# A LayerNorm / RWKV / mixture-of-experts block on one Trainium2 core: the first channel-mix steps are written between the last time-mix steps on every engine, and two waits of the early shared-expert units move

## What is computed

```python
h  = layernorm(x) * (1 + ca) + sa
# attention part: a time-mix and a channel-mix
g  = layernorm(h, ln1);  gp = shift(g)                    # shift by one row
r  = sigmoid(mix(g, gp, mu_r) @ Wr);  k = mix(..mu_k) @ Wk;  v = mix(..mu_v) @ Wv
x1 = h + (r * exp(u + k) * v / (exp(u + k) + 1e-8)) @ Wout        # time-mix
g2 = layernorm(x1, ln2); g2p = shift(g2)
r2 = sigmoid(mix(g2, g2p, mu_r2) @ Wr2)
k2 = square(relu(mix(g2, g2p, mu_k2) @ Wk2))
x  = x + ga * (x1 + r2 * (k2 @ Wv2))                       # channel-mix
# feed-forward part: 2 shared halves and 8 experts of 352, two experts a row
h3 = layernorm(x) * (1 + cb) + sb
x  = x + gb * (sum over top-2 experts + shared)(h3)
```

## Time and profile before

| | |
|---|---|
| median of 3 runs | 1848.51 us (1846.16 to 1848.79) |
| profiled execution: its time, its span | 1840.96 us, 1839.2 us |
| PE busy | 1712.8 us, 93% |
| DVE, ACT, POOL busy | 1344.8, 772.1, 547.4 us |
| mean granted TensorE clock | 0.971 of full |
| time-mix ends, channel-mix begins | near 463 us |
| EARLY part | 1071 to 1136 us |

### The profile page before, as it was taken

One profiled execution on the slowest core, in us unless ns is written; L12 is line 12 of the kernel. 1 busy time (PEld: TensorE's weight loads), 2 busy tenths in 40 slices (PEclk: granted clock), 3 DMA queues, 4 the chain that ended last, 5 costly groups with the idle time before them and its releaser, 6 DMA issues.

```text
span 1839.2 us, 28387 instructions
## 1 busy us (share of the span) xinstructions
PE 1712.8 (93%) x9093; PEld 1485.2 (81%) x9093; DVE 1344.8 (73%) x2468; ACT 772.1 (42%) x1151; POOL 547.4 (30%) x631
## 2 busy tenths in 40 slices
PE   5499999999579999999999988999999999999998
PEld 0388888887468888888887878999999999998898
DVE  4899999995578778787877545666666767665872
ACT  2343333332245545454554313545455454542331
POOL 0244444442254433545554540000000000003740
PEclk9699999999889999999999979999999999999999
DMA  9432222221533443545454688677777777675861
GB/s 334 134 118 91 85 80 86 91 80 60 178 115 123 157 146 115 212 172 178 172 195 149 207 302 296 229 266 262 260 250 247 272 244 274 232 250 165 294 217 43
DMA packets 141638, 339.30 MB, mean 184 GB/s; under 512 B 20664, under 2 KB 20664, under 8 KB 136048
## 3 DMA queue, kind: packets, MB, share of 16 engines
q1 hardware_dynamic: 110864, 250.68, 39.8%
q10 hardware_dynamic: 20448, 54.01, 7.9%
q0 software_dynamic: 10240, 33.56, 5.3%
HBM read 230.40 MB, written 107.79 MB: 184 GB/s over the span
## 4 chain that ended last, share of the span: by engine, by line
PE 65%; DVE 19%; DMA 5%; issue 4%; POOL 3%; ACT 2%; SPq 1%; DVEq 0%; ACTq 0%; POOLq 0%
PE bank L573 16%; PE bank L575 16%; PE bank L574 16%; DVE mix L1570 5%; PE bank L584 4%; PE bank L2074 4%; PE bank L2072 4%; PE bank L2073 4%; PE bank L2067 2%; DVE xm_lo L1576 1%; ACT xm_hi L1173 1%; POOL diff L1017 1%; DMA stage<-in_w_k 1%; DVE hid L1654 1%; POOL raw L1107 1%
## 5 line engine op out<-in xcount | busy, mean ns | idle before, releaser
L573 PE MATMUL bank<-gu_hi,ex_x_hl 128*128 128x352 f32 x1136 | 380.7, 335 | 3.8 <-DMA ex_x_hl<-h_turned 2.0
L575 PE MATMUL bank<-gu_hi,ex_x_hl 128*128 128x352 f32 x1136 | 368.7, 325 | 0.0
L574 PE MATMUL bank<-gu_lo,ex_x_hl 128*128 128x352 f32 x1136 | 368.6, 324 | 0.0
L1107 POOL DMA_INDIRECT raw<-expert_out_rows,out_slots x64 | 73.9, 1154 | 596.6 <-DMA expert_out_rows<-y_rows 572.6
L1654 DVE TENSOR_TENSOR hid<-bank,sg_t 128x352 f32<-128x352 f32 x142 | 74.0, 521 | 200.4 <-ACT sg_t L1231 200.4
L573 PEld LDWEIGHTS bank<-gu_hi,ex_x_hl 128*128 128x128 f32 x1136 | 215.9, 190 | 4.4 <-DMA ex_x_hl<-h_turned 2.2
L574 PEld LDWEIGHTS bank<-gu_lo,ex_x_hl 128*128 128x128 f32 x1136 | 216.2, 190 | 0.0
L1570 DVE SCALAR_TENSOR_TENSOR mix<-diff,vecs,h2T 128x128 f32<-128x128 f32 x256 | 160.7, 695 | 75.6 <-POOL diff L1017 75.6
L575 PEld LDWEIGHTS bank<-gu_hi,ex_x_hl 128*128 128x128 f32 x1136 | 215.5, 190 | 0.0
L1231 ACT ACTIVATE sg_t<-bank 128x352 f32<-128x352 f32 x142 | 66.1, 466 | 273.5 <-PE bank L575 273.2
L2072 PE MATMUL bank<-dn_hi,hid_hi 128*128 128x512 f32 x426 | 170.3, 400 | 8.1 <-DVE hid_lo L1658 8.1
(11 more groups left out here) (231 smaller groups left out, 3941.0 us busy)
## 6 DMA issues: line engine op xcount, KB each, us to landing
raw<-in_ex_gu SPq DMA_DIRECT2D x39, 1408.0 KB, 6.8
raw<-in_ex_dn SPq DMA_DIRECT2D x39, 512.0 KB, 7.5
ex_x<-expert_in_rows SPq DMA_DIRECT2D x78, 256.0 KB, 2.8
expert_out_rows<-y_rows ACTq DMA_DIRECT2D x78, 256.0 KB, 4.2
h_rows<-h_t SPq DMA_DIRECT2D x64, 256.0 KB, 2.4
h_turned<-h_hl ACTq DMA_DIRECT2D x32, 512.0 KB
ex_x_hl<-h_turned ACTq DMA_DIRECT2D x32, 512.0 KB, 3.8
x_t<-in_x SPq DMA_DIRECT2D x32, 256.0 KB, 2.6
```

Of the source, the lines that this page charges most:

```text
L573: pe.matmul(acc, act_hi[i], w_hi[i], start=(i == 0), stop=False)
L574: pe.matmul(acc, act_hi[i], w_lo[i], start=False, stop=False)
L575: last = pe.matmul(acc, act_lo[i], w_hi[i], start=False, stop=(i == chunks - 1))
L1107: pool.indirect_dma_start(rows[:, pair % 2, a, :], None, ys_d, bass.IndirectOffsetOnAxis(ap=out_slots[:, k, n:n + 1], axis=0)).then_inc(ar ...
```

## The change

`with_units` is gone. `time_mix` runs the time-mix up to step 28 (`JOIN = 29`), and `joined` writes out the rest: time step n, and behind it the channel steps up to `CHANNEL_UP_TO[n]`. So channel steps -4 and -3 stand behind time step 29, -2 behind 30, -1 behind 31, 0 behind 33 and 1 behind 34, on each engine as far as it has such steps. The waits that stood between the stages move into the channel step that needs them. The small tiles `st2`, `mv2`, `var2`, `rstd2` get room of their own, and `o`'s result and `t1`'s trade banks (`PS_T1`, `PS_O`). SP loads the first two `x2` tiles in time step 28. On PE the last time step is written by hand: `trw(31)`, `r2(0)`, `o(31)`. In the EARLY part the load of tile 15 is issued in unit 27 (which takes the wait for the last `xh` along), and the wait for `mod3_in` stands in `base_of(15)`.

```diff
+JOIN = 29
+CHANNEL_UP_TO = {29: -2, 30: -1, 31: 0, 32: 0, 33: 1, 34: 2}
...
+def joined(lead, lag, time_step, channel_step):
+
+    done = -lead
+    for n in range(JOIN, NT + lag):
+        time_step(Tile(None, n, NT))
+        for s in range(done, CHANNEL_UP_TO[n]):
+            channel_step(Tile(None, s, NT))
+        done = max(done, CHANNEL_UP_TO[n])
+    for s in range(done, STEPS + 1):
+        channel_step(Tile(None, s, NT))
...
-        PS_R, PS_K, PS_O, PS_T1, PS_TR = psum[0:5]
+        PS_R, PS_K, PS_T1, PS_O, PS_TR = psum[0:5]
...
-                if t.pair is None and t.n == NT - 2:
+                if t.only(JOIN - 1):
                     sp.wait_ge(*lnh_vec.done(NT - 1, "h"))
                     for n in range(2):
                         load_x2(Tile(None, n, NT))
...
-                if v.pair is None and v.n == 2 * FU - 1:
-                    act.wait_ge(*xh2_vec.done(NT - 1, "xhat"))
-                    load_turned(EARLY, FU)
+                if v.n == 2 * FU - 1:
                     load_turned(EARLY, FU + 1)
                 else:
                     fused_turned(v.half + 1)
+                if v.n == 2 * FU - 3:
+                    act.wait_ge(*xh2_vec.done(NT - 1, "xhat"))
+                    load_turned(EARLY, FU)
...
             def base_of(part, n):
+                if n == FU:
+                    dve.wait_ge(mod3_in, 16 * B)
...
                         if t.only(FU):
                             base_fused(FU - 1, 2 * FU - 1, True)
-                            dve.wait_ge(mod3_in, 16 * B)
...
+            def time_step_with_r2(t):
+                if t.only(NT + 1):
+                    trw(t.back(2))
+                    r2(Tile(None, 0, NT))
+                    o(t.back(2))
+                else:
+                    time_step(t)
+
+            joined(2, time_lag, time_step_with_r2, channel_step)
```

More of the change, by code:

```diff
@@ L170, in sweep, with time_mix @@
         body(Tile(None, t, count, first))
+def time_mix(eng, lead, lag, body):
+    low = lag + 2 + lag % 2
+    high = min(NT - lead, JOIN) // 2 * 2
+    for t in range(-lead, low):
+        body(Tile(None, t, NT))
+    with eng.Fori(0, (high - low) // 2) as k:
+        for j in range(2):
+            body(Tile(k, low + j, NT))
+    for t in range(high, JOIN):
+        body(Tile(None, t, NT))
+def joined(lead, lag, time_step, channel_step):
[7 more added lines that the diff above has]
+        channel_step(Tile(None, s, NT))
 def sweep_part(eng, part, lead, lag, body):
@@ L266, in build @@
         pad_row = tables.put("pad_row", [P, E], I32)
+        st2 = tables.put("st2", [P, 2, 6])
+        mv2 = tables.put("mv2", [P, 2, 2])
+        var2 = tables.put("var2", [P, 2])
+        rstd2 = tables.put("rstd2", [P, 2, 1])
         assert tables.at <= consts.at
@@ L366, in build @@
         h3_hl = second.put("h3_hl", [P, 2, C, P], F32R)
[L367 to L370, removed]
         st3 = second.put("st3", [P, 2, 6])
@@ L854, in channel_step_and_rows @@
             def channel_step_and_rows(t):
+                if t.only(0):
+                    sp.wait_ge(*rkv_pe.done(NT - 1, "v"))
+                    sp.wait_ge(zero_out, 16 * SPARE)
                 channel_step(t)
                 load_next_scattered(t)
-            with_units(lead, channel_step_and_rows)
+            joined(lead, time_lag, time_step, channel_step_and_rows)
             def load_last_scattered(n):
@@ L998, in rw @@
                 pool.tensor_tensor(rw_t, vk_t, sr_t[t.p], ALU.mult).then_inc(rw_pool.sem, 1)
[L1000 to L1004, removed]
+            time_lead, time_lag, time_step = in_turn((diff, -1), (x_rstd, -4), (rw, 1), (h_rstd, -3))
+            time_mix(pool, time_lead, time_lag, time_step)
             def rstd_2(t):
@@ L1072, in channel_step_and_scatter @@
             def channel_step_and_scatter(t):
+                if t.only(-2):
+                    wait_h_rows(pool)
+                    pool.wait_ge(*t1_pe.done(NT - 1, "turned"))
+                    pool.memset(h2T[:, 1, :, P:P + 1], 0.0).then_inc(const_ready, 1)
                 channel_step(t)
                 scatter_ready(t)
-            with_units(lead, channel_step_and_scatter)
+            joined(lead, time_lag, time_step, channel_step_and_scatter)
             pool.wait_ge(*y_vec.done(NT - 1, "y"))
@@ L1281, in channel_step_and_exp @@
             def channel_step_and_exp(t):
+                if t.only(-2):
+                    wait_h_rows(act)
                 channel_step(t)
                 route_exp_of(group_at(t.n, 0))
-            with_units(lead, channel_step_and_exp)
+            joined(lead, time_lag, time_step, channel_step_and_exp)
             def hidhi_before(part, t, half):
@@ L1533, in x2_of @@
                 dve.tensor_tensor(hin_t[:, t.p, :], PS_O[:], hin_t[:, t.p, :], ALU.add).then_inc(x2_vec.sem, 1)
[L1535 to L1541, removed]
+            time_lead, time_lag, time_step = in_turn(
+                (first_col, -1), (z_of, 1), (x2_of, 3), (x_stats, -4), (scaled, -3), (hhat, -2), (h_of, -3),
+                (x_moments, -4), (split_last, -1), (mixes, -1), (h_stats, -3), (vk_of, 1), (rwlo, 2), (h_moments, -3),
+                (split_staged, -3), (mix_lo, -1))
+            time_mix(dve, time_lead, time_lag, time_step)
             def stats_2(t):
@@ L1753, in one_step @@
             def one_step(t):
+                if t.only(-1):
+                    wait_h_rows(dve)
+                    dve.wait_ge(const_ready, CONSTS + 1)
                 for stage_of, lag in ((logits_out, 3), (routing(3, row_slots), None), (routing(0, less_max), None),
@@ L2003, in o @@
                         chunks_of(lo["o"])).then_inc(rw_pe.sem, 1)
-            sweep(pe, NT, *in_turn((r, 0), (trw, 2), (k, 0), (t1, -2), (v, 0), (o, 2)))
+            time_lead, time_lag, time_step = in_turn((r, 0), (trw, 2), (k, 0), (t1, -2), (v, 0), (o, 2))
+            time_mix(pe, time_lead, time_lag, time_step)
             def t2(t):
@@ L2009, in t2 @@
                     pe.wait_ge(*h2T_act.done(t.back(1).n, "h2T"))
+                else:
+                    pe.wait_ge(*h1T_act.done(NT - 1, "h1T"))
                 if t.back(4).real():
@@ L2017, in r2 @@
                     pe.wait_ge(*post2_act.done(t.back(1).n, "sr2"))
+                else:
+                    pe.wait_ge(*sr_act.done(NT - 1, "sr"))
                 pe.wait_ge(*mix2_vec.done(t.n, "mix_lo"))
@@ L2128, in rank_in_step, with later_r2 @@
                     rank(g)
-            lead, _, before_rank = in_turn((r2, 0), (k2, 0), (fused_up, LAG), (tk, 0), (t3, 2), (fused_down, LAG), (cv, 0))
+            def later_r2(t):
+                if not t.only(0):
+                    r2(t)
+            lead, _, before_rank = in_turn((later_r2, 0), (k2, 0), (fused_up, LAG), (tk, 0), (t3, 2), (fused_down, LAG), (cv, 0))
             _, _, after_rank = in_turn((router, 2), (t2, -2))
@@ L2136, in channel_step @@
                 after_rank(t)
-            with_units(2, channel_step)
+            def time_step_with_r2(t):
[3 more added lines that the diff above has]
+                    o(t.back(2))
+                else:
+                    time_step(t)
+            joined(2, time_lag, time_step_with_r2, channel_step)
             def weights_of(part, t, half):
```

16 lines of the change are left out of this document (6 added, 10 removed).

## The result

| | before | change |
|---|---|---|
| median | 1848.65 us (4 runs, 1846.16 to 1850.95) | 1825.12 us (4 runs, 1822.41 to 1826.80) |
| profiled execution: time, span | 1840.96, 1839.2 | 1823.68, 1821.9 |
| mean granted clock | 0.971 | 0.972 |

The ratio is 0.9872, 95% interval 0.9852 to 0.9891: 23.5 us between the medians. Between the two profiled executions it is 17.3 us, for which the prediction had 16.9.

What follows compares the result with a forecast made beforehand. PE was taken as the bound, busy 93% of the span, with gains only where it idles or runs at half clock. 11.6 + 5.3 = 16.9 us off the 1848.51 median gave 1831.6 us, 8-in-10 range 1824 to 1839.5.

Steps and rivals of the forecast that it cites:

- The seam: Between time-mix and channel-mix: PE's idle time shrinks, so tile 0's relu starts at 471.5 instead of 483.1, 11.6 us gained.
- The chain of 6.9 us: At the seam: from the start of `diff` to the end of `xh(1)` takes 6.9 us, as before, done at 453.4.
- the queue order's 3 us: At the seam: channel-mix work queued ahead on ACT and DVE starts `o(30)` 3.0 us later, at 457.9 instead of 454.92.
- the 1.7 of low clock: At the seam: after two PE waits the clock is low, 3.4 us at half rate, losing 1.7 us; bounds none and 11.2.
- the rival in which it meets POOL: At the seam: tile 0's mix collides with POOL's work, +3.0 on `xh(1)` and `o(30)`; gain 13.9, 1834.6 us, chance 0.06.
- The 0.2 until ACT may read: At the seam's end: ACT may read 0.2 us after PE's products, so the relu of tile 0 starts at 471.5.
- everything behind depends on tile 0's and 1's steps, so it moves with them: Behind the seam: later work shifts with the first two tiles' steps, keeping the whole 11.6 us.
- I put the same gain on the median: Whole time: the 16.9 us worked out on the profiled execution is also taken off the median, 1848.51 to 1831.6.
- the EARLY term: EARLY part: PE comes 11.3 us earlier, gathered rows only 7.4, and 2.1 is lost to the clock: net 5.3 us.
- The DMA engines do not bind: Rival: the routed start comes all 11.3 us earlier and the seam's clock holds; up to 24.6 gained, 1823.9 us, chance 0.10.
- EARLY gives nothing: Rival: SP's chain comes no earlier, PE waits 13 us at ROUTED; 9.5 us gained, 1839.0 us, chance 0.12.
- the change does nothing or makes it slower: Two rivals: the wait only moves, within 3.7 us of before, 0.04; or `stats_2` of tile 2 delays PE, slower, 0.04.

Runs made afterwards that it cites:

- the change with the extra store: The change plus one more 2.1 MB store of zero rows on SP, ahead of the zero rows; 1828.18 us in one execution.
- the change with the weights ahead: The change with SP loading the second expert's weights ahead of the wait for the zero rows; 1825.29 us, ratio 0.9867 to the kernel before.
- the new seam order: The change with the last tile's small time-mix work ahead of the channel-mix chain; 1825.7 us, ratio 0.9862 to the kernel before.

## Why the prediction was right, and what it missed

**The seam.** Forecast: `t2(1)` at 453.6, `o(30)` at 457.9, the relu at 471.5. Measured: 453.90, 458.15, 471.60. The chain of 6.9 us and the queue order's 3 us held, and so did the 1.7 of low clock (from `o(30)` to the next transpose 4.42 us instead of 2.80, at a granted clock of 0.61). The mix of tile 0 took 2.19 us, with POOL idle from the end of `diff` at 447.85 until 453.40, so the rival in which it meets POOL did not occur. The 0.2 until ACT may read held too: matmuls follow one another at 0.23, so the last of `k2(0)`, at 471.17, takes until 471.40, and the relu starts at 471.60. The step "everything behind depends on tile 0's and 1's steps, so it moves with them" looks 2 us too generous between the two profiled executions: the gain rose to 12.6 at tile 3 and fell to 9.7 by tile 5 and 9.5 by tile 31, behind like waits of PE, by the clock. The windows above have it at 0.57 and 0.72; those of before at the same work are

```profile
538.60:546.60 8.00, 6.46 (x28) 5.47 (x29) 7.83 (x13) 0.68 (x2) 4.19 (x4) 0.79 0.49 184
558.00:564.00 6.00, 5.67 (x31) 4.90 (x32) 5.83 (x12) 1.30 (x4) 2.42 (x3) 1.00 0.53 193
```

But the change did not cause this. Before's second execution has the low values at that work, and the change with the extra store, whose seam is the change's own, has the high ones:

```profile
538.30:546.30 8.00, 6.44 (x21) 5.31 (x22) 7.83 (x13) 0.00 (x0) 4.18 (x4) 0.57 0.46 176
558.90:564.90 6.00, 5.62 (x24) 4.71 (x25) 5.85 (x11) 0.00 (x0) 2.46 (x3) 0.72 0.54 190
```

```profile
528.30:536.30 8.00, 7.02 (x31) 5.91 (x32) 7.82 (x14) 1.25 (x4) 4.42 (x4) 0.79 0.55 199
546.80:552.80 6.00, 5.35 (x30) 4.61 (x31) 5.86 (x10) 1.08 (x4) 2.74 (x3) 1.00 0.50 176
```

Between executions with the same clock there, the seam's gain at tile 31 is 10.7 us (the extra-store run against the first execution of before) and 11.9 (the change against the second), around the 11.6 forecast. What gives an execution the one clock or the other stays open.

**EARLY.** PE came 11.3 us earlier to `base_of(15)` (from 9.5 to 20.8), as forecast. The gathered rows, less that 9.5, came 7.9 earlier, where 7.4 was forecast from 9.86 MB at 401 GB/s, and PE's wait at ROUTED was 4.61 where I had 5 to 6. Net it gave 6.3 instead of 5.3. That `mod3` would be just in time for `base_of(15)` was right as well, and the trace with 1.26 us of wait shows the other side of it. From 1087 to 1100 the DMA engines moved 405 GB/s. At the 401 GB/s of rows 11 the extra 2.1 MB last 5.2 us, and 5.2 were measured.

**The sum.** 16.9 forecast, 17.3 measured on the profiled executions. That they agree so closely is partly luck: the 2.1 us that the clock took from the seam's gain in this pair were made up by EARLY's 1.0 and by 1.5 more behind it that the forecast didn't have. The step that was off was the last one: "I put the same gain on the median". It was 23.5, 6.6 more. By the halves measured alone it is above all the EARLY term that is too small for the median: 5.3 forecast, 10.9 measured (interval 8.3 to 13.3), while the seam's 11.6 is inside its interval (13.3, 10.7 to 15.7). The profiled execution of the change lies 1.4 us below its median, but the first one of before 7.7 below: its second is 1852.05, its runs, on two chips, go from 1839.05 to 1856.11, and its medians beside the experiments from 1845 to 1850. The first one had a short wait behind `mod3`. The waits for tile 15's rows and behind `mod3` together are 6.3 us in it; in the three other profiled executions with the `mod3` wait in its old place they are 8.1, 8.6 and 9.7 or more. The change leaves 0 to 3.2 us of them, so it would gain more in an ordinary execution than in that one. Laid on before's second execution, the EARLY edits' 5.7 becomes 9.8 (+4.1 by the end of ROUTED) and the seam's 9.5 becomes 11.9 (+2.4 of clock); measured alone were 10.9 and 13.3. These 6.5 us would cover the 6.6, but this is argued and not shown: it rests on two executions of before, the second is 3.4 us above the median and its 4.6 us in LATE are left out of the count, and other kernels spread too (the change with the weights ahead from 1817.56 to 1828.30). How much of before's spread each wait makes, and why `mod3` lands as it does, stays open.

**The rivals.** "The DMA engines do not bind" has the time nearest to the measured median (1823.9 against 1825.1; the forecast had 1831.6), but is wrong as a mechanism: the added store and PE's waits of 4.61 and 5.83 us show that they bind. That EARLY gives nothing is excluded by its 10.9 us alone; that the change does nothing or makes it slower, by the ratio.

## What to carry to other kernels

Lay the new order of each in-order queue on the old timestamps: it gave the start of `o(30)` and of the relu within 0.3 us. Where two waits follow one another, removing the first alone gives nothing (here 0.9998 against 0.9941 for both). Take the gain from the profiled execution but ask how ordinary that execution is: a wait that the change removes may be 4 us in one and 10 in the next, and the clock behind equal waits may differ by 3 us, so a second profile of before is worth more than a finer sum.

## What the runs showed of the hardware

- After like waits of PE (3.8 to 4.0 and 2.1 us, in steps 3 and 4) the granted clock was 0.57 and 0.72 in some executions and 0.79 and 1.00 in others over the same work, with the kernel before and with the change's seam alike. It moved the gain by 3 us.
- At the start of LATE, PE stood 3.65 and 1.5 us in the second execution of before, and 3.80 us in that of the new seam order, for nothing the profile names; ACT stood 6.41 us "remote" before the `sg_t` that PE needed. In the first execution of before PE stood 0.81 us there, behind DVE. This costs 4 to 6 us in some executions; its cause is open.
- DMA engines at a share of 1.04 moved 405 GB/s over 13 us for one core, with PE at full clock and 92% busy beside them.
